# Grouped attention as one stream of 512 units, with the heads of later pairs and the score maxima placed beside them

## What is computed

```python
xn = _layernorm(x, ln_scale, ln_bias)
q = (xn @ Wq).reshape(b, n, HEADS, d).transpose(0, 2, 1, 3)
kv = xn @ Wkv
k, v = jnp.split(kv, 2, axis=-1)
k = k.reshape(b, n, g, d).transpose(0, 2, 1, 3)
v = v.reshape(b, n, g, d).transpose(0, 2, 1, 3)
q = _layernorm(q, qn_scale, qn_bias)
k = _layernorm(k, kn_scale, kn_bias)
qg = q.reshape(b, g, hg, n, d)
dots = jnp.einsum('bghqd,bgkd->bghqk', qg, k) * scale
attn = jax.nn.softmax(dots, axis=-1)
out = jnp.einsum('bghqk,bgkd->bghqd', attn, v)
out = out.transpose(0, 3, 1, 2, 4).reshape(b, n, g * hg * d)
return out @ Wout
```

## Time and profile before

| what | us |
|---|---|
| median of 3 runs | 6802.32 |
| the runs | 6792.39, 6803.70, 6802.32 |
| profiled execution, its own time | 6793.93 |
| its span (first to last instruction) | 6792.1 |
| mean granted clock of TensorE in the span | 0.90 of 2.4 GHz |
| PE, DVE, ACT, POOL busy in the span | 5957.6, 4574.7, 3310.4, 4234.6 |

### The profile page before, as it was taken

The page is one execution under the profiler, slowest core; times in us unless marked ns, Lnnn a source line. Parts: engine busy times, 40 slices in busy tenths (PEclk is TensorE's granted clock), DMA queues, the critical chain, the costliest instruction groups (busy, mean ns, idle before and its releaser), DMA issues. The chain is left out here.

```text
span 6792.1 us, 188444 instructions
## 1 busy us (share of the span) xinstructions
PE 5957.6 (88%) x75387; PEld 4031.7 (59%) x75387; DVE 4574.7 (67%) x5380; ACT 3310.4 (49%) x3775; POOL 4234.6 (62%) x2000
## 2 busy tenths in 40 slices
PE   8998986888988888889899889889868888888887
PEld 4334335776766667655555555555357667666665
DVE  5335437888888888775545545455178888888886
ACT  1431344666666666513323333333346666666664
POOL 0000007888888888516567657667878788887884
PEclk6765668999999999989899889889989999999999
DMA  0000002222222222100000000000022222222221
GB/s 24 1 1 1 1 1 68 68 65 71 68 67 67 67 63 66 51 9 1 1 2 1 1 2 1 1 1 1 1 68 73 66 71 62 72 64 70 65 67 50
DMA packets 187287, 254.59 MB, mean 37 GB/s; under 512 B 59996, under 2 KB 80984, under 8 KB 186200
## 3 DMA queue, kind: packets, MB, share of 16 engines
q1 hardware_dynamic: 186392, 242.02, 13.7%
HBM read 38.98 MB, written 1.57 MB: 6 GB/s over the span
## 5 line engine op out<-in xcount | busy, mean ns | idle before, releaser
L1813 POOL TENSOR_TENSOR XB<-XB,Pb 128x1024 f32<-128x1024 f32 x448 | 1086.7, 2426 | 284.9 <-ACT Pb L1771 259.7
L913 POOL TENSOR_TENSOR sin_qk<-raw_qk,rot 128x512 f32<-128x512 f32 x768 | 1001.8, 1325 | 81.6 <-ACT raw_qk L821 50.8
L1865 DVE TENSOR_REDUCE b_pmax<-slot 128x1 f32<-128x1024 f32 x512 | 621.5, 1223 | 611.8 <-PE slot L1607 611.6
L1771 ACT ACTIVATE Pb<-slot 128x1024 f32<-128x1024 f32 x512 | 505.0, 1026 | 951.7 <-PE slot L1634 887.9
L929 POOL TENSOR_TENSOR rot_out<-rot_out,sin_qk 128x1024 f32<-128x1024 f32 x192 | 596.2, 3105 | 362.4 <-DVE rot_out L987 361.3
L946 POOL TENSOR_TENSOR inv_norm<-norm2c,minus_half 128x16 f32<-128x16 f32 x192 | 668.9, 3484 | 171.4 <-DVE norm2c L1088 171.1
L286 POOL TENSOR_TENSOR rstd<-variance,minus_half 128x4 f32<-128x4 f32 x20 | 19.8, 1009 | 1075.3 <-DVE variance L295 1075.2
L535 PE MATMUL slot<-w_hi,x_hi 128*128 128x512 f32 x1152 | 544.8, 473 | 67.1 <-POOL w_lo L904 44.4
L942 POOL TENSOR_TENSOR inv_norm<-norm2c,minus_half 128x16 f32<-128x16 f32 x192 | 559.2, 2912 | 0.0
L786 ACT ACTIVATE qT<-slot 128x1024 f32<-128x1024 f32 x192 | 197.3, 1028 | 704.2 <-PE slot L542 704.2
L987 DVE TENSOR_TENSOR rot_out<-slot,rot 128x1024 f32<-128x1024 f32 x384 | 468.6, 1220 | 65.6 <-PE slot L542 28.5
(11 more groups left out here) (223 smaller groups left out, 13344.3 us busy)
## 6 DMA issues: line engine op xcount, KB each, us to landing
VW<-V SPq DMA_DIRECT2D x1152, 128.0 KB
VW<-V SPq DMA_DIRECT2D x768, 64.0 KB
w_raw<-in_Wqkv SPq DMA_DIRECT2D x36, 512.0 KB, 3.6
Wo<-in_Wo SPq DMA_DIRECT2D x12, 512.0 KB, 4.1
W<-in_W SPq DMA_DIRECT2D x12, 341.0 KB, 3.2
consts<-in_shape_constants SPq DMA_DIRECT2D x1, 2436.5 KB, 8.7
W<-in_W SPq DMA_DIRECT2D x24, 64.0 KB
out<-out_nat SPq DMA_DIRECT2D x2, 512.0 KB, 3.4
```

The costliest lines, as they stand in the source:

```text
L913: ins = pool.tensor_tensor(dst[:, :, x, :], src[:, :, 1 - x, :], tab, ALU.mult)
L1771: act.activation(Pb[:, n % B_RING, :], slot[n % 2][:, :], ACT.Exp).then_inc(s["b_exp"], 1)
L1813: pool.tensor_tensor(b_sum[:, qb % 2, :], Pb[:, (n - 1) % B_RING, :] if k == 1 else b_sum[:, qb % 2, :], Pb[:, n % B_RING, :], ALU.add).th ...
L1865: dve.tensor_reduce(b_pmax[:, n // 2, n % 2:n % 2 + 1], o[:, :], AX.X, ALU.max).then_inc(s["b_max"], 1)
```

## The change

- The 8 pairs are one written-out stream of 512 units; the hardware loop over groups is gone, and the work between pairs with it.
- Heads are worked one block of 512 columns at a time in the free half of slot 3 (`HEAD`), beside units 7 to 15 of a window (`pe_beside`, `act_beside`, `pool_beside`, `dve_beside`). A window has up to two of them: `first`, a block of keys (only beside even pairs 0, 2 and 4), and `second`, a block of queries of the pair after next. HEAD is shared with `sums`, `project`, the transposed maxima and the values, so PE waits at units 7 to 15 until the reader before is done.
- Centring moves from DVE to ACT, which copies and squares out of PSUM.
- The maxima are combined, transposed and written out in blocks of 8 rows (one query block), one window later each, 32 times in place of 8.
- SP (`sp_grouped`) waits for the parts of each such block, writes them to DRAM and reads them back, in 6 DMAs a block.
- KA, KB and Vb have two buffers each, so the copies from KA_next and KB_next are gone; weights are read where they lie, so the copies into b_w and b_wo are gone.
- Maxima of pair 0 go through three slots, with the queries of pair 1, the values of group 0 and the first three blocks of maxima beside them. Two layer norms, keys of group 0 and queries of pair 0 stay ahead.

The numbers of score units, maxima units and head blocks (512, 512 and 48) stay as they were.

```diff
-        KA = sb("KA", [128, S], F32R, mem)
-        KB = sb("KB", [66, S], F32R, mem)
-        KA_next = sb("KA_next", [128, S], F32R, mem)
-        KB_next = sb("KB_next", [66, S], F32R, mem)
-        Vb = sb("Vb", [128, NCH, 64], F32, mem)
+        KA = [sb(f"KA{i}", [128, S], F32R, mem) for i in range(2)]
+        KB = [sb(f"KB{i}", [66, S], F32R, mem) for i in range(2)]
+        Vb = [sb(f"Vb{i}", [128, NCH, 64], F32, mem) for i in range(2)]
...
+        HEAD = slot[3][:, 512:1024]
+        FIRST = -1
...
+        def heads_beside(p, w):
+            if w < 0:
+                p, w = p - 1, w + NB
+            if p < FIRST:
+                return None, None
+            keys = ("k", p // 2 + 1, w) if p >= 0 and p % 2 == 0 and p < PAIRS - 2 else None
+            if p == FIRST:
+                queries = ("q", 1, w)
+            else:
+                queries = ("q", p + 2, w - 1) if w else ("q", p + 1, NB - 1)
+                if queries[1] >= PAIRS or queries[1] == 1:
+                    queries = None
+            return keys, queries
...
+        def pe_head(pe, head, o):
+            kind, i, b = head
+            if kind == "q":
+                mm = pe.matmul(o, b_wq[:, 128 * i:128 * i + 128], z2[:, block_columns(b)], start=True, stop=True)
+            else:
+                for r in range(2):
+                    mm = pe.matmul(o[64 * r:64 * r + 64, :], b_wkv[:, 64 * i:64 * i + 64], z2[:, block_columns(b)],
+                                   start=True, stop=True)
+            mm.then_inc(s["ln_mean"], 1)
...
+        def act_head(act, head, o):
+            act.wait_ge(s["ln_mean"], norms_to(head))
+            act.activation(centred[:, columns_of(head)], o, ACT.Copy).then_inc(s["ln_centred"], 1)
+            act.wait_ge(s["ln_var"], norms_to(head) - 2)
+            act.activation(squares[:, nth(head) % 2, :], o, ACT.Square).then_inc(s["ln_square"], 1)
...
+        def pe_beside(pe, p, n):
+            k, w = n % 16, n // 16
+            first, second = heads_beside(p, w)
+            m, v = maxima_before(p, w), values_beside(p, w)
+            last = NB * p + w - 1
+            before = norms_before_window(p, w)
+            if k == 7:
+                if last >= 0:
+                    pe.wait_ge(s["b_invd"], START + 4 * (last + 1))
+                pe.wait_ge(s["ln_half"], before)
+                if first:
+                    pe_head(pe, first, HEAD)
+            if k == 8 and second:
+                if first:
+                    pe.wait_ge(s["ln_square"], norms_to(first))
+                pe_head(pe, second, HEAD)
+            if k == 9:
+                if second:
+                    pe.wait_ge(s["ln_square"], norms_to(second))
+                elif first:
+                    pe.wait_ge(s["ln_square"], norms_to(first))
+                if first:
+                    pe_head_variance(pe, first, HEAD)
+            if k == 10 and last >= 0:
+                if first:
+                    pe.wait_ge(s["ln_eps"], norms_to(first))
+                project(pe, last)
+            if k == 11:
+                if last >= 0:
+                    pe.wait_ge(s["b_yadd"], START + last + 1)
+                if first:
+                    pe.wait_ge(s["ln_eps"], norms_to(first))
+                if second:
+                    pe_head_variance(pe, second, HEAD)
+            if k == 12 and m is not None:
+                if second:
+                    pe.wait_ge(s["ln_eps"], norms_to(second))
+                pe.wait_ge(s["b_comb"], START + m + 1)
+                pe.transpose(slot[3][0:8, 512:640], b_nmax[:, 8 * (m % NB):8 * (m % NB) + 8], ident)\
+                  .then_inc(s["b_nt"], 1)
+            if k == 13:
+                if m is not None:
+                    pe.wait_ge(s["b_los"], START + m + 1)
+                elif second:
+                    pe.wait_ge(s["ln_eps"], norms_to(second))
+                if first:
+                    pe.wait_ge(s["ln_pow"], norms_to(first))
+                    pe_head_spread(pe, first, HEAD)
+            if k == 14 and v:
+                if first:
+                    pe.wait_ge(s["ln_half"], norms_to(first))
+                kv, half = v
+                for x in range(8):
+                    t0 = 1024 * half + 128 * x
+                    mm = pe.matmul(HEAD[:, 64 * x:64 * x + 64], z2[:, t0:t0 + 128],
+                                   b_wkv[:, 256 + 64 * kv:320 + 64 * kv], start=True, stop=True)
+                mm.then_inc(s["b_v"], 1)
+            if k == 15:
+                if v:
+                    pe.wait_ge(s["b_vsb"], START + 2 * v[0] + v[1] + 1)
+                elif first:
+                    pe.wait_ge(s["ln_half"], norms_to(first))
+                if second:
+                    pe.wait_ge(s["ln_pow"], norms_to(second))
+                    pe_head_spread(pe, second, HEAD)
+        def project(pe, last):
+            pe.wait_ge(s["b_on"], START + last + 1)
+            pe.wait_ge(s["b_invd"], START + 4 * (last + 1))
+            pe.matmul(HEAD, b_wout[:, last // NB, :], Ob[:, :], start=True, stop=True).then_inc(s["b_y"], 1)
...
+            for p in range(PAIRS):
+                for n in range(0, B_UNITS, 2):
+                    at = B_UNITS * p + n
+                    pe_beside(pe, p, n)
+                    maxima(p, n)
+                    scores(p, n)
+                    scores(p, n + 1)
+                    pe_beside(pe, p, n + 1)
+                    maxima(p, n + 1)
+                    if at:
+                        values(at - 2)
+                        values(at - 1)
+                    if at >= 16 and n % 16 == 2:
+                        sums(at // 16 - 1)
...
+        def act_beside(act, p, n, before):
+            k, w = n % 16, n // 16
+            first, second = heads_beside(p, w)
+            m, v = maxima_before(p, w), values_beside(p, w)
+            if not before and k == 0 and heads_beside(p, w - 1)[1]:
+                act_head_high(act, heads_beside(p, w - 1)[1])
+            if not before and k == 7 and first:
+                act_head(act, first, HEAD)
+            if before and k == 8 and second:
+                act_head(act, second, HEAD)
+            if before and k == 12 and m is not None:
+                act.wait_ge(s["b_nt"], START + m + 1)
+                act.wait_ge(s["b_rows"], START + 32 * m)
+                act.activation(b_hi[:, :], slot[3][0:8, 512:640], ACT.Copy, scale=-1.0).then_inc(s["b_his"], 1)
+            if before and k == 14 and v:
+                kv, half = v
+                act.wait_ge(s["b_v"], START + 2 * kv + half + 1)
+                act.activation(Vb[kv % 2][:, 8 * half:8 * half + 8, :].rearrange("p k d -> p (k d)"), HEAD, ACT.Copy)\
+                   .then_inc(s["b_vsb"], 1)
+            if not before and k == 14 and first:
+                act_head_high(act, first)
...
+        def pool_beside(pool, p, n):
+            k, w = n % 16, n // 16
+            first, second = heads_beside(p, w)
+            if k == 10 and first:
+                pool_head(pool, first)
+            if k == 12 and second:
+                pool_head(pool, second)
+                pool.wait_ge(s["ln_pow"], norms_to(second))
+                pool.sem_inc(s["passed"], 1)
+                pool_no_maxima(pool, second[1], second[2])
...
+        def dve_beside(dve, p, n, before):
+            k, w = n % 16, n // 16
+            first, second = heads_beside(p, w)
+            m, last = maxima_before(p, w), NB * p + w - 1
+            if before:
+                if k == 0 and m is not None:
+                    dve_combine(dve, m)
+                if k == 9 and first:
+                    dve_head_eps(dve, first, HEAD)
+                if k == 10 and last >= 0:
+                    add(dve, last)
+                if k == 11 and second:
+                    dve_head_eps(dve, second, HEAD)
+                if k == 12 and m is not None:
+                    dve.wait_ge(s["b_his"], START + m + 1)
+                    dve.scalar_tensor_tensor(out=b_lo[:, :], in0=slot[3][0:8, 512:640], scalar=-1.0,
+                                             in1=b_hi[:, :].bitcast(F32), op0=ALU.mult, op1=ALU.subtract)\
+                       .then_inc(s["b_los"], 1)
+                if k == 13 and first:
+                    dve_head_scale(dve, first, HEAD)
+                if k == 15:
+                    if first:
+                        dve_head_low(dve, first)
+                    if second:
+                        dve_head_scale(dve, second, HEAD)
+            else:
+                if k == 1 and heads_beside(p, w - 1)[1]:
+                    dve_head_low(dve, heads_beside(p, w - 1)[1])
+                if 3 <= k < 7 and last >= 0:
+                    invert(dve, last, k - 3)
+                if k == 7 and last >= 0:
+                    scale(dve, last)
+                if k == 13 and first:
+                    dve_head_affine(dve, first)
+                if k == 15 and second:
```

(10 more changed lines are left out.)

616 lines of the change are left out of this document (264 added, 352 removed).

## The result

The changed kernel takes 6705.1 us (median of four, 6694.3 to 6713.2), beside 6803.0 for the kernel before. The ratio is 0.9858, with a 95% interval of 0.984 to 0.9876. The forecast was 6586, with a range of 6550 to 6670: the gain is 98 us, not 216.

A forecast was written before the change was run, and what follows sets the result against it. PE was taken to bound the windows, with 323 us between pairs to save less 139 moved inside: 184, plus 31 before pair 0 and 1 in the last pair, 216 in all; 6586 us forecast, range 6550 to 6670.

The forecast's parts named there:

- The view of the bound: Windows with maxima beside them are bound by PE alone, 48.2 us each; the other engines have room.
- The prices of heads, values and transposed maxima: PE work moved into the windows of pairs 0 to 6: heads 105 us, values 11, transposed maxima 7.
- The wait at unit 7: In every window PE waits at unit 7 for DVE's fourth inverse: 0.6 us, 27 times, 16 us.
- A rule that speaks against it: DVE's two-SBUF-operand instructions and POOL's additions slow each other at most 0.6 us each, against the skill's rule of exclusion.
- case 2: Rival: DVE waits out POOL's additions in the windows; PE loses some 3 us a block, 108, time 6694; chance 0.08.
- Case 5: Rival: PE's clock falls to its lower level within the stream, slower than before, 6958 us at half; chance 0.03.
- Before pair 0: Ahead of pair 0's first exponent: 19 us saved around the first maxima, 12 in the heads ahead, together 31.
- Both stacks stay as they are: The two layer stacks, before and after the grouped attention, do not change in time.
- The last pair: Pair 7 is set by POOL at the same 2.55 us an addition; 1 us saved.

The follow-up runs named there:

- additions thinned: Changed kernel with GpSimd's additions cut to one column everywhere but the first of windows 0 and 1, so denominators leave out nearly all probabilities: 6605.6 us, ratio 0.9735.
- freed and mended one: Changed kernel with DVE's two-operand and copying SBUF instructions beside the pairs replaced or moved to ACT and POOL, plus two mends (key waits, last pair's scaling): 6637.2 us, ratio 0.9764.
- one variant: Changed kernel with the maximum of the two halves' maxima taken by a one-operand reduction instead of two operands in SBUF: 6715.1 us, ratio 0.9867.

## Why the prediction was wrong, step by step

- *The view of the bound* was right. Windows without heads stay at 48.8 us, windows with heads are PE's where DVE is not held, and SP's small DMAs were never waited for.
- *The prices of heads, values and transposed maxima* were right. With the additions thinned, a window of two heads lasts 54.84 us where the terms make 48.2 + 5.86 + 0.25 + 0.6 = 54.9 (0.6 for the wait at unit 7, which took 0.32), one of one head 51.7 (52), and a half of the values adds 53.53 - 51.72 = 1.8 (11 in all). Two key halves do run side by side.
- *The wait at unit 7* was there, with half the size: 0.32 us in each of 27 windows, 9 in place of 16.
- **The step that failed first** is the paragraph "A rule that speaks against it", and with it the chance of 0.08 for case 2. I read a scale of 0.78 us amid POOL's additions as proof that the two don't wait out each other. The rows say the opposite. The groups of the kernel before (durations min/median/max) are

```profile
L1890 DVE TENSOR_TENSOR Ob<-Oc,b_inv x32: 692/1205/1348, 3152.6 to 4917.2; 128x512 f32<-128x512 f32 x32
...
L1813 POOL TENSOR_TENSOR XB<-XB,Pb x448: 2337/2407/2752, 3091.4 to 4909.3; 128x1024 f32<-128x1024 f32 x150
```

  The row of additions began at 4799.66, and its first ended at 4802.05. The scale began at 4801.82, 0.23 us ahead of that end and not in the middle of the addition, and ended at 4802.60, 0.55 behind it. In the changed kernel the low part ended 3426.50 - 3425.95 = 0.55 behind the addition. The scale follows the sums, which follow an addition, so in the kernel before it met the next one only near its end: the 24 that did took 0.78 to 1.35 us, where the low parts of the changed kernel took up to 2.80. A sample from there says nothing of what an instruction at another place meets. The maximum in the group, 1348 ns, is no bound for the same reason, and so the 0.6 us an instruction that I drew from it was none. By the Trainium skill, "SBUF — State Buffer", section "SBUF: two separate sides", the shared pair of ports "is an **exclusive lock**, not a bandwidth split", and of a GpSimd instruction and a DVE one with two SBUF inputs or in a mode that uses both ports, the one that starts first keeps the pair to its end. The traces now agree, down to the exceptions: a head's scale with an operand in PSUM (a mean near 0.68 us) and the reduction of one operand (172 ns) are not held.
- *The second thing missing in the pairs is the clock.* Over the 27 windows the changed kernel takes 1508.8 us and the one with thinned additions 1431.1. Of the 77.7 between them 44.8 are idle time of PE and 33.0 are busy time. The changed kernel spends 44 us of these windows at the lower level, which makes 22 of the 33, the same matmuls at half the clock; the other 11 lie in windows at 1.00 too and stay unexplained. Case 5 argued that the change leaves no idle time of the length that comes before 0.50 (9.15 us). Waits of 1.4 to 1.6 us are enough, in 11 of 24 windows. What decides in which of them is open. The thinned kernel, with no wait over 0.32 us there, and the freed and mended one, with none over 0.64, stay at 1.00 in all 27.
- *Case 2's price* of 108 was too high by a third: 75 us were lost, clock included. That its 6694 lies near the 6705 measured is in part chance, as the stack's 30 us and the 16 ahead of pair 0 are not in it.
- *Before pair 0* the 31 us came out as 15 (14.6 and 14.4 in the table; 190.0, 186.6 and 186.5 us in the profiles of before's order, 169.6 to 175.6 in the others). The heads ahead took 39.7 us, where the same stretch took 42.4: 2.7 saved in place of 12, because DVE's low parts of the first queries stand end to end behind the last head.

```profile
2975.48 1.40 DVE L1665 TENSOR_TENSOR QA<-normed,QA 64x512 fp32r<-64x512 f32 x2
2976.91 0.42 DVE L1667 CAST QB<-QA 64x512 fp32r<-64x512 f32 x1
...
2982.56 0.42 DVE L1667 CAST QB<-QA 64x512 fp32r<-64x512 f32 x1
2982.91 2.34 DVE L1951 TENSOR_REDUCE b_pmax<-slot 128x1 f32<-128x1024 f32 x2
```

  The first maxima with heads beside them took 98.6 us, not 92.4. DVE was busy for 85.7 of them and idle for 12.9, in waits for PE of 0.2 to 1.5 us, where I had added 4.
- *"Both stacks stay as they are"* failed by 30 us in the second one in these two profiles, by some 24 over all of them, as shown above. The first stack's 14.6 us are not put down to the change. Three profiles of before's order began the attention at 2893.3, 2912.1 and 2901.9 us, and those of the changed order at 2899.9 to 2929.4.
- *The last pair* was right: 1.8 us saved, POOL-bound windows of 37.7 us.

## What to carry to other kernels

When work moves to an engine that shares SBUF's ports with another, sort its instructions by where their operands lie, and give the ones with two operands there, or copies within it, a place where nobody waits, or another engine. Before a single short duration is taken as proof, find where in the other engine's instruction it fell, and look at the median of its group. Code that is written out shifts every loop behind it, so compare the untouched stages too.

## What the hardware showed that I had not expected

- A wait of PE of only 1.4 to 1.6 us, in a stream at 1.00 before it, was followed in 11 of 24 windows (20 of 24 in one variant) by some 3.4 us at the lower clock, which costs 1.7 us, as much again as the wait.
- An instruction on 8 columns took 2.35 us, since it began just after an addition had.
- Sixty-four empty instructions ahead of a loop made the stretch with it some 19 us shorter in the changed kernel and 8 to 11 longer in the one before, and 256 left it as it was. The Trainium skill, "Runtime: NRT & Kernel Launch", section "Instruction fetch mechanics", says that instructions are fetched in blocks of 256 and that a taken branch breaks the prefetch. The return with 256 (1910 us, one profile) would fit that, but 192 gave 1907 as well. Whether the 133 to 162 us of issue idle time in PE's 1887 to 1921 are such fetches no run here shows.
